# Windowed attention and DCT gating over eight images: strips written out, rows and taps spread anew, and each image's first pieces moved into the image before

## What is computed

```python
freq = abs(dct2(x))                                  # once for all images: a noise mask
noise_mask = ...                                     # from freq, one 96 x 96 map per image
# attention in windows of 12 x 12 pixels (L = 144), 8 heads of 32 channels
qkv = win @ qkv_w.T + qkv_b
attn = softmax(q @ k.T * SCALE + bias)
x_attn = (attn @ v) @ proj_w.T + proj_b
# depthwise 3 x 3 convolution, nine taps per pixel
x_lpe = (conv2d(x, lpe_w, groups=C, pad=1) + lpe_b) * lpe_scale * noise_mask
a = x_attn + x_lpe
freq2 = dct2(a)
gate = sigmoid(5.0 * (abs(freq2) - freq2.mean(axis=(2, 3))))
y = batchnorm(conv2d(x + idct2(freq2 * gate), fr_w)) # 1 x 1; statistics over all 8 images
return gelu(y)
```

## Time and profile before

| what | value |
|---|---|
| median of 3 runs | 8906.17 us (8887.17 to 8919.15) |
| the profiled execution | 8901.16 us |
| its span, first to last instruction | 8899.5 us |
| mean granted clock of TensorE | 0.929 of 2.4 GHz |
| TensorE, matmuls busy | 8087.5 us, 91% |
| VectorE | 5500.7 us, 62% |
| ScalarE | 5125.3 us, 58% |
| GpSimd | 2717.2 us, 31% |

### The profile page before, as it was taken

How to read it: one execution, slowest core, us unless ns; L and a number is a source line. 1 busy time by engine, 2 the same in 40 slices (tenths; PEclk the granted TensorE clock), 3 DMA queues, 4 the chain that set the end, 5 groups by cost and what they waited for, 6 DMA issues and landing times.

```text
span 8899.5 us, 253693 instructions
## 1 busy us (share of the span) xinstructions
PE 8087.5 (91%) x84778; PEld 6050.9 (68%) x84778; DVE 5500.7 (62%) x20355; ACT 5125.3 (58%) x16576; POOL 2717.2 (31%) x3673
## 2 busy tenths in 40 slices
PE   9998999999999999999999999999999999999930
PEld 8996666866676667666686667666766667666720
DVE  4554787467845875377746784588547764678410
ACT  5554775466644774377546664577537753666434
POOL 1211443133422443144313442244314431334200
PEclk9998998999999998999899999999899989999865
DMA  7561000200012000200020001200020002000089
GB/s 125 98 108 38 15 21 22 77 17 21 15 38 65 20 21 15 86 15 21 22 82 13 21 15 39 66 18 21 15 86 15 21 21 85 12 19 15 25 331 410
DMA packets 386919, 487.12 MB, mean 55 GB/s; under 512 B 249617, under 2 KB 352529, under 8 KB 369297
## 3 DMA queue, kind: packets, MB, share of 16 engines
q1 hardware_dynamic: 369488, 393.67, 15.4%
q0 software_dynamic: 16192, 77.49, 2.2%
HBM read 319.45 MB, written 151.66 MB: 53 GB/s over the span
## 4 chain that ended last, share of the span: by engine, by line
PE 75%; issue 15%; DMA 4%; POOL 3%; DVE 2%; ACT 1%; POOLq 1%; SPq 0%; DVEq 0%; ACTq 0%
PE ps L952 65%; PE ps L1090 5%; POOL work L472 3%; DMA AH<-y_scratch 2%; PE ps L1135 2%; PE ps L1087 2%; DMA out<-AH 1%; PE ps L1088 1%; DVE work L807 1%; POOLq L469 0%; DVE work L771 0%; DVE work L817 0%; ACT AH L662 0%; ACT work L561 0%; DVE work L679 0%
## 5 line engine op out<-in xcount | busy, mean ns | idle before, releaser
L561 ACT ACTIVATE work<-work 128x144 f32<-128x144 f32 x5120 | 2042.7, 403 | 38.0 <-issue 37.2
L952 PE MATMUL ps<-work 32*32 32x144 f32 (+3 forms) x32902 | 1754.7, 302 | 159.8 <-issue 97.6
L771 DVE CUSTOM_DVE_ANT_0 work<-ps,negbias 128x144 f32<-128x144 f32 x5120 | 1247.1, 302 | 628.9 <-issue 430.2
L807 DVE SCALAR_TENSOR_TENSOR work<-xs,lw,work 128x570 f32<-128x570 f32 (+1 forms) x2048 | 1588.3, 812 | 0.0
L952 PEld LDWEIGHTS ps<-work 32*32 32x32 f32 (+2 forms) x32902 | 999.8, 127 | 770.7 <-issue 643.6
L952 PE MATMUL ps<-work,wqkv 128*128 128x288 f32 x4096 | 1325.8, 448 | 101.6 <-POOL work L453 83.7
L438 POOL TENSOR_TENSOR work<-work 128x80 f32<-128x80 f32 x1024 | 483.1, 472 | 3054.0 <-DVE work L778 3054.0
L441 POOL TENSOR_TENSOR work<-work 128x640 f32<-128x640 f32 x1024 | 1310.2, 1279 | 0.0
L952 PEld LDWEIGHTS ps<-work,wqkv 128*128 128x128 f32 x4096 | 738.5, 198 | 391.6 <-POOL work L432 88.0
L561 ACT ACTIVATION_READ_ACCUMULATOR work<-work 128x1 f32 x5120 | 973.2, 190 | 0.0
L952 PE MATMUL ps<-dct,AH 96*96 96x97 f32 (+1 forms) x7168 | 823.0, 269 | 9.7 <-ACT AH L495 9.2
(11 more groups left out here) (127 smaller groups left out, 11793.7 us busy)
## 6 DMA issues: line engine op xcount, KB each, us to landing
work<-in_x SPq DMA_DIRECT2D x128, 576.0 KB, 5.5
xs<-in_x SPq DMA_DIRECT2D x64, 1152.0 KB, 5.3
AH<-in_x SPq DMA_DIRECT2D x192, 384.0 KB, 3.4
y_scratch<-AH SPq DMA_DIRECT2D x192, 384.0 KB, 2.5
AH<-y_scratch SPq DMA_DIRECT2D x64, 1152.0 KB, 23.6
out<-AH POOLq DMA_DIRECT2D x64, 1152.0 KB, 17.4
xs<-in_x SPq DMA_DIRECT2D x112, 96.0 KB, 5.2
bias_scratch<-in_rpb_rev POOLq DMA_DIRECT2D x144, 4.5 KB, 2.1
```

What stands on the lines that cost most here:

```text
L561: o = act.activation(sp[t % 4][:, c, :], sp[t % 4][:, c, :], ACT.Exp, scale=-1.0, bias=mn[t % 4][:, c:c + 1], accum_out=den[t % 4][:, c:c ...
L771: v.tensor_tensor_reduce(out=sp[t % 4][:, c, :], in0=psS[c], in1=negbias[:, t % 2, c, :], scale=1.0, scalar=BIG, op0=ALU.add, op1=ALU.min, ...
L807: v.scalar_tensor_tensor(dst[:, ct, :, w0:w1], xs[side][:, ct, y0 + dy:y0 + dy + HS, w0 + dx - 1:w1 + dx - 1], lw[:, ct, tap:tap + 1], dst ...
L952: return nc.tensor.matmul(o, l, r, start=start, stop=stop)
```

## The change

1. `each_strip` writes the six inner strips out, with no loop over them. `each_image` loops over the first seven images and writes the last one out.
2. `row_at` lays the twelve rows into steps 2 to 13. One buffer `rowt` stands in place of two, so `row_masked` waits until the row before was added; in the closing rows the odd ones use `sp[0]`.
3. `taps_at` gives both halves of a strip to this strip itself, eight steps each, in every strip, the head too. Three half buffers `lpe` go round.
4. The prologue of image b+1 stands in the y stage of image b, before the branch. GpSimd cuts its windows behind the frequency stage. TensorE puts piece 0 before y group 22, piece 1 before group 23, and pieces 2 to 5 behind it, each in a bank of its own (0 to 5). The common wait for the stores and statistics goes on TensorE, ScalarE and GpSimd; VectorE makes its statistics, does its part of the prologue and then waits for the stores. In `work` the buffers of the prologue lie clear of what the y stage still reads.
5. `b1_out` makes two copies, of 384 and of 4 columns, so that `f2` reads its operand without gaps.
6. ScalarE runs a one-column Exp between the frequency and the y stage.

The diff, cut to its core; the same change of `attention` and `image` is made on each of the four engines:

```diff
         def row_at(t):
-            return t - 2 if 2 <= t < 8 else t - 4 if t >= 10 else None
+            return t - 2 if 2 <= t < 2 + WS else None
...
-        def taps_at(t, head, last):
-            share = lambda i, n: list(range(18 * i // n, 18 * (i + 1) // n))
-            if t < 8:
-                return [] if head else [(1, k) for k in share(t, 8)]
-            if not last:
-                return [(0, k) for k in share(t - 8, 8)]
-            return [(0, k) for k in share(t - 8, 5)] if t < 13 else [(1, k) for k in share(t - 13, 3)]
+        def taps_at(t):
+            half, i = t // 8, t % 8
+            return [(half, k) for k in range(18 * i // 8, 18 * (i + 1) // 8)]
+        def each_image(eng, image):
+            if B > 1:
+                with eng.Fori(0, B - 1) as b:
+                    image(b, False)
+            image(B - 1, True)
         def each_strip(eng, strip):
             strip(0, 0, head=True)
-            with eng.Fori(0, NS // 2 - 1) as i:
-                strip(i * 2 + 1, 1)
-                strip(i * 2 + 2, 0)
+            for s in range(1, NS - 1):
+                strip(s, s % 2)
             strip(NS - 1, 1, last=True)
...
 # ScalarE
-                    act.activation(b1[par][0:96], ps[0:96, par, 0:388].rearrange("p (c l) -> p c l", l=97),
+                    f1 = ps[0:96, par, 0:388].rearrange("p (c l) -> p c l", l=97)
+                    act.activation(b1[par][0:96, 0:384].rearrange("p (c l) -> p c l", l=96), f1[:, :, 0:96], ACT.Copy)
+                    act.activation(b1[par][0:96, 384:388], f1[:, :, 96:97].rearrange("p c l -> p (c l)"),
                                    ACT.Copy).then_inc(S["b1_ready"], 1)
...
+                    still = lambda: None
+                    attention(b + 1)(0, 0, first=True, between=(still, y_late(0), y_late(1), still, still, still))
...
 # VectorE, row_masked
                         v.wait_ge(S["row_ps"], m * WS + r + 1)
+                        if not ends or r:
+                            v.wait_ge(S["a_row"], m * WS + r + (0 if ends else 1))
...
 # TensorE, piece
-                        if i:
+                        if i >= NPC:
                             pe.wait_ge(S["piece_out"], n * (NP * NPC) + i)
...
 # TensorE, end of an image
+                    still = lambda: None
+                    free = lambda: pe.wait_ge(S["z_ready"], b * NG + NG - 1)
+                    freed = lambda: pe.wait_ge(S["y_ready"], b * NG + NG - 1)
+                    attention(b + 1)(0, 0, first=True, between=(free, y_late(0), y_late(1), still, freed, still))
```

More of the change, by code:

```diff
@@ L353, in image @@
                            (S["agg_step"], b * 7 + 7))
[L355 to L358, removed]
+            each_image(sy, image)
             def load_f(b, first):
@@ L461, in strip, with image @@
                             windows(t // 4 + 2)
-                strip(0, 0, first=True)
-                each_strip(g, strip)
+                return strip
+            def image(b, ends):
+                each_strip(g, attention(b, False))
                 g.wait_ge(S["norm_done"], (b * (NS * NT) + NS * NT) * 2)
@@ L474, in _ @@
                                         ALU.subtract).then_inc(S["tg_ready"], 1)
-                for par in range(2):
-                    g.wait_ge(S[f"y_out{par}"], b * (NG * 8) + NG * 8)
-                g.wait_ge(S["agg_step"], b * 7 + 7)
+                if not ends:
+                    attention(b + 1, True)(0, 0, first=True)
+            attention(0, False)(0, 0, first=True)
+            each_image(g, image)
             with g.Fori(0, B) as b:
@@ L530, in _, with attention, strip @@
             act.wait_ge(S["m_done"], 1)
-            with act.Fori(0, B) as b:
-                def strip(s, par, head=False, last=False, first=False):
+            def attention(b):
+                def strip(s, par, head=False, last=False, first=False, between=((lambda: None),) * NPC):
                     n = b * NS + s
@@ L603, in strip, with image @@
                         o_out(NT - 1)
-                strip(0, 0, first=True)
-                each_strip(act, strip)
+                return strip
+            def image(b, ends):
+                each_strip(act, attention(b))
                 act.wait_ge(S["o_out"], b * (NS * NT) + NS * NT)
@@ L844, in strip @@
                             scores_out(t + 3)
-                        steps = taps_at(t, head, last)
-                        last_half = last and t >= 13
+                        steps = taps_at(t)
                         r = None if head else row_at(t)
@@ L925, in _ @@
                 v.tensor_copy(ag[:, 0, 0:1], ag[:, 0, 1:2]).then_inc(S["agg_step"], 1)
+                v.wait_ge(S["agg_step"], base + 7)
+                if not ends:
+                    attention(b + 1)(0, 0, first=True)
                 for par in range(2):
                     v.wait_ge(S[f"y_out{par}"], b * (NG * 8) + NG * 8)
-                v.wait_ge(S["agg_step"], base + 7)
+            attention(0)(0, 0, first=True)
+            each_image(v, image)
             f = [0]
@@ L1023, in _, with attention, strip @@
             pe.wait_ge(S["setup_vec"], 2)
-            with pe.Fori(0, B) as b:
-                def strip(s, par, head=False, last=False, first=False):
+            def attention(b):
+                def strip(s, par, head=False, last=False, first=False, between=((lambda: None),) * NPC):
                     n = b * NS + s
@@ L1125, in attend_few, with row @@
                         last.then_inc(S["av"], 1)
-                    def row(m, r, bank, side, ends=False):
+                    def row(m, r, bank, side):
                         if r == 0:
@@ L1142, in strip @@
                     if first:
+                        for i, beside in enumerate(between):
+                            beside()
+                            piece(i)
+                        pe.wait_ge(S["piece_out"], n * (NP * NPC) + HG)
                         pe.wait_ge(S["q_pad"], b * 6 + 6)
-                        for i in range(4):
-                            piece(i)
                         for t in range(3):
@@ L1191, in strip, with image @@
                                 pe.wait_ge(S["a_row"], n * WS + r - 2)
-                            row(n, r, r % 4, par, ends=True)
+                            row(n, r, r % 4, par)
                         pe.wait_ge(S["a_row"], n * WS + WS + 1)
-                strip(0, 0, first=True)
-                each_strip(pe, strip)
+                return strip
+            def image(b, ends):
+                each_strip(pe, attention(b))
                 mmul(ps[0:96, psM, 0:1], eye[:, 0:96], eye[:, 0:1]).then_inc(S["image_done"], 1)
```

150 lines of the change are left out of this document (87 added, 63 removed).

## The result

The changed kernel takes 8448.1 us (median, 8434.6 to 8463.3) against 8896.7 of the kernel before beside it, a ratio of 0.9495 with a 95% interval of 0.9466 to 0.9524: 5.1% faster, where 4.1% was forecast. The forecast was 8540, with a range of 8440 to 8650. The profiled execution has a span of 8432.9 us.

The account below looks back on a forecast made before the run. TensorE, busy 91% of the span, bounds the kernel, so gains lie where it idles, waits or runs at its lower clock. Terms 86 + 18 + 133 + 129 = 366 off 8901 give 8535, 8540 on the median's scale; range 8440 to 8650.

Parts of the forecast that it names:

- the four places named: Per image: seam between images, branches between inner strips, last strip's steps 8 to 15, and the frequency stage's first 27.3 us.
- rival 1: Frequency stage keeps its clock because the tail's idle TensorE goes: some 70 us more gained, 8470 us; chance 0.16.
- Written-out strips: Inner strips: two backward branches per image go, with 10.7 us for each four strips holding both; 86 us gained.
- Rows: Strips: two rows move from steps 14, 15 to 8, 9, at most 36 us gained in 56 strips; 18 taken.
- The added wait: One row buffer: masking a row waits for the add of the row before, a whole step later; cost 0.
- Taps: Head takes eighteen new taps at cost 0; last strip's steps 8 to 15 fall from 49.3 to 33.6 us; 133 us gained.
- Seam: Between images: last y matmul to first transposition falls from 41.5 to 23.5 us, 21 less in the seventh; 129 us gained.
- half-clock allowance: Between images: 21.1 us at full clock, 24.9 at the lower one from the first scores on; 23.5 taken.
- The frequency stage: Split copy and operand without gaps cost or gain 0; its first 27.3 us at clock 0.50 were left unchanged.
- The fetch rival: Written-out strips are held up by instruction fetch, so the branch holes return: 8626 us; chance 0.06.
- The clock that stays down through a head strip: After the seam 1.2 GHz holds through each head, some 61 us more each: 8970 us, slower than before; chance 0.03.
- Rivals 4 and 5: Tail and seam give only lower bounds, 8630 us; or next image's pieces don't start early, 8613; together 0.13.

Follow-up runs that it names:

- a_rows_old: The changed kernel with the rows back in steps 2 to 7 and 10 to 15: 8456.6 us, ratio 0.9529.
- a_again: The changed kernel run once more with nothing changed: 8455.8 us, ratio 0.9519 to the kernel before.
- a_images_out: The changed kernel with all eight images written out, no image loop: 8407.0 us, ratio 0.9469 to the kernel before.
- a_tail_old: The changed kernel with the last strip's taps laid as in the kernel before: 8519.7 us, ratio 0.9590 to the kernel before.
- b_unrolled: The kernel before with its six inner strips written out, nothing else changed: 8764.7 us, ratio 0.9866.
- b_rows: The kernel before with the twelve rows in steps 2 to 13, nothing else changed: 8815.9 us, ratio 0.9931.
- b_fill_start: The kernel before with three unread matmuls per image at the frequency stage's start: 8796.1 us, ratio 0.9895.

## Why the prediction was right

**What bounds the kernel.** Right: the four places named hold nearly all of the change. TensorE's strips without a hole moved by what was taken from them and by 0.65 us more. The profiles have 467 us gained where the sum has 366. The 101 between them are 66 in the frequency stage, 42 in the inner strips and 10 in the first prologue, less 2 in the seams, 5 in the tail and 10 at the start of y. On the medians the forecast is 92 us too high, 9 of them because the kernel before took 8897 beside the changed one and not 8906. The range held by 8 us at its lower end, and 70 of the 100 us that it reached down were those of rival 1, whose cause is wrong: that part is luck.

**Written-out strips, 86 us.** The holes were sized right, and straight code has none. The term was too small: a strip in the loop is 0.65 us slower than the same strip written out, which no row of before showed, as it holds no inner strip outside the loop. Measured 118.

**Rows, 18 us.** Measured 24 in the 48 inner strips (a_rows_old), 28 if the heads and last strips' share is put at the same 0.5 us, between the bounds. Four steps each, of the first inner strip after, beside the earlier trace rows:

```profile
1833.00:1851.60 18.60, 18.27 (x237) 12.76 (x237) 15.16 (x70) 14.43 (x57) 8.07 (x12) 1.00 0.23 76
1851.60:1871.90 20.30, 20.30 (x249) 14.53 (x248) 17.26 (x70) 14.17 (x54) 8.44 (x12) 1.00 0.01 2
1871.90:1892.20 20.30, 20.30 (x249) 14.52 (x248) 16.88 (x71) 14.16 (x54) 8.46 (x12) 1.00 0.01 3
1892.20:1910.30 18.10, 18.10 (x238) 12.54 (x235) 15.26 (x65) 13.81 (x54) 8.40 (x12) 1.00 0.01 3
```

The last four, with rows in their first two steps, take 18.1; 16.29 + 1.81 says the same. Adding the cost of a row by its place in the four steps was the right way, and halving the result was caution without a reason. The added wait on the one row buffer shows in none of these rows; no run took it out alone.

**Taps.** The head's steps 0 to 7 took none of it: heads behind no branch take 63.1 and 64.7 us. The tail was forecast at 33.6 us and takes 33.9 to 35.7 in the images; with the closing rows 128 us, forecast 133. The single steps came out too: steps 8 to 11 take 19.9 us (forecast 19.6), step 12 3.9 (4.3), step 13 3.5 (3.5), step 14 3.0 (2.3) in a_again.

**Seam, 129 us.** Measured 127 in the seven seams, 10 more in the first image's prologue. The way there was wrong in one term: I gave the branch 3.5 us of an idle TensorE, and it shows 1.04 (that TensorE takes its branch beside the work of the other engines is my reading and was not tested). Most of its cost is paid in the head behind it, which takes 66.5 us instead of the 63.1 without a branch (a_images_out). So the branch costs some 4 us with the clock behind it; that 3.5 us and the half-clock allowance came to the right sum was partly luck.

**The frequency stage, 0 us.** This is the step that failed, and the largest part of the miss in the profiles. I wrote that 27.3 us at 0.50 would stay because the stage's start stays. The start does stay, and the drop with it, in all eight images: with three fillers at the start it is gone, in both kernels. What didn't stay is its length, which I had read off one image and priced as fixed. In the profile before the drops last 27.3 us in five images and 41.0 to 44.4 in three; in the changed kernel 6.8 to 34.1, and 6.8 to 41.0 in a_again, whose stages are only 38 us below the 1227. Rival 1 named the size and had the wrong cause; the old tail put back (a_tail_old) leaves the stage as it is. Nor is the gain shown to be the change's: b_unrolled and b_rows leave this stage alone and take 1199 and 1160. The 1227 are one profiled execution, at 8901 us and a mean clock of 0.929, while the kernel before elsewhere took 8853 to 8919 at up to 0.936. What sets the length, and whether the kernel before meets long drops more often, is open.

**The other rivals.** The fetch rival is out by b_unrolled. The clock that stays down through a head strip didn't come: heads lose some 3 us. The Trainium skill ("TensorE: Matmul & The Clock Gate", Part 1) has activity release the throttle. The heads fit that: the low stretch from the seam ends some 5 us into a head of 66.7 us. In the frequency stage TensorE was fully busy through 27.3 us at 0.50, and there the measurement decides. Rivals 4 and 5 didn't come.

## What to carry to other kernels

Where TensorE is the bound, look for its short waits at the start of a stage before its work: behind waits of 1.2 and 1.6 us per image stood low stretches that cost 115 us in eight images, and three matmuls that nobody reads took them away. Look at where the drop begins in each image, too: in the second image it was the 1.66 us wait, in the third the 1.19. A loop costs more than its branch: price the body too, by one copy of it outside. When a stretch at the lower clock is seen once per image, compare it over all images and over two profiles before calling it a cost of what stands ahead of it.

## What the runs showed of the hardware

- A backward branch between strips left TensorE 3.48 us without work, and strips in the loop took 78.5 us against 77.8 written out. In the changed kernel the image loop's going took them from 77.3 to 76.9.
- The granted clock fell to 0.50 within 10 us of the frequency stage's start in every image of every kernel without fillers there: either within 2 us behind a wait of 1.6 us or, earlier, some 2 us behind a wait of 1.2 us, before any wait of 1.6 us (4 of 8 images in the kernel before, 3 of 8 in the changed one). With one matmul behind the first wait and two in the second it fell in no image, in both kernels (b_fill_start: 1112 us of frequency stages where 1227 stood).
- How long it then stays down scatters in one program: from 3.4 to 44.4 us within b_unrolled, so that the same 64 turns take 141 to 157 us. In one of 44.4 us, in the third image of the kernel before, TensorE was busy for 44.2.
